# Four plain blocks ahead of the first causal one, and x carried between its two blocks through DRAM

## The chip, the core and the metric

The kernel runs on one core of a Trainium2 chip. The metric is the device time of one execution in microseconds. The program has five engines that run side by side and meet at semaphores: TensorE (PE, with its weight loads listed as PEld), VectorE (DVE), ScalarE (ACT), GpSimd (POOL) and SyncE (SP), which here does nothing but issue DMAs and wait for what they need.

## The reference

The input x has 8 batch elements of 512 rows by 256 columns. Each element passes through two blocks of the same form:

```
x = x + attention_a(layernorm(x))     # 16 heads of 16, all 512 keys, with biases
x = x + tree_ffn(layernorm(x))
x = x + attention_b(layernorm(x))     # 16 heads of 16, rotary, causal, no biases
x = x + tree_ffn(layernorm(x))
```

The tree layer projects to 255 gates, multiplies the branch probabilities of a binary tree of 8 levels into 256 leaf weights, and multiplies those with a matrix of leaf values and an output matrix (folded into one matrix, as are the gates' two, when the kernel opens). Elements do not depend on each other. The first two lines are a *plain* block here, the last two a *causal* block: its scores exist only on and below the diagonal, so it has fewer columns to compute.

## The kernel before, in words

**Phases.** The work is 16 phases, one a block: 8 plain and 8 causal. causal(n) and element(n) (L151 to L160) say what phase n is. With AHEAD = 3 the order is P P P C P C P C P C P C P C C C: phases 0, 1, 2 are the plain blocks of elements 0, 1, 2; phases 3, 5, 7, 9, 11 are causal blocks of elements 0 to 4; phases 4, 6, 8, 10, 12 are plain blocks of elements 3 to 7; phases 13, 14, 15 are the causal blocks of elements 5, 6, 7.

**Slots.** A phase has 64 slots; in each, every engine does its share of one step: PE one block of scores by key (L1104), ACT its exponential (L750, 512 columns or fewer when causal), PE a product with the values (L1128, in fours). Scores for the row maximum (PE L1082, DVE L842 when plain, L838 when causal) run 28 slots ahead (LEAD), so phase n's slots 36 to 63 compute the maxima of phase n + 1, and PE cannot start on them before the stacked queries and keys of n + 1 have landed.

**Work around the slots.** Beside the slots of phase n runs work of other blocks, each step at a due slot of hand-written tables. FINISH (L73) ends block n - 1: its attention output is turned, projected out and added to x (project_out, slots 18 to 23), then layernorm (slots 21 to 28), gates, tree, and the second addition (mix, slots 58 to 63). PREPARE (L85) begins a block m: the layernorm steps (moments, spread, normalize, turn_normed, slots 37 to 55) in phase m - 2, and its heads, splits into three bf16 parts and stacks (slots 1 to 23) in phase m - 1. The split parts are moved into q_stack and k_stack by SP: 12 DMAs for a plain block (L494), 24 for a causal one (L492). SP also sends 4 small rows four times a phase (send_shift, L481, slots 6, 22, 38 and 54). Every engine walks the same tables in program order, so a wait on SP holds all its later DMAs.

**Late blocks.** A causal block of an element needs the output of its plain block, whose mix ends at slot 63 of the phase after it. ready_late(m) (L173) names the blocks for which the input is not there at slot 37 of phase m - 2, or that have no such phase: m = 1, 3 and 15. For them LATE (L108) puts the layernorm steps at slots 0 to 8 of phase m - 1, the heads at slots 9 to 20, and every other step but values 9 slots later (LATE_BY).

**Buffers of x.** x_in takes the input of a plain block for its layernorm, loaded at slot 10 of phase m - 2 (load_x, L455); x_again takes it once more for the addition, loaded at slot 40 of phase m (load_again, L462, for plain blocks), and gets the output bias on POOL (bias_input, L664, plain blocks only). Results are added into x_plain or x_causal by DVE (L900). Between its two blocks an element stays on chip: move (L534) copies x_plain to x_moved, keep (L548) copies x_moved to x_kept, the keep at slot 24 (KEEP_SLOT) and the move at slot 31 (MOVE_SLOT) of phases 4, 6, 8, 10, 12, with two more moves and one more keep after the first two mixes: 7 moves and 6 keeps. A causal block's layernorm reads x_moved (x_plain when late), its addition x_kept. A causal block's result is stored by SP after its mix (L591).

```
FINISH = (
...
    ("mix", 0, (58, 59), 60), ("mix", 1, (61, 62), 63),
PREPARE = (
    ("moments", 0, (), 37 - SLOTS), ("moments", 1, (), 38 - SLOTS), ("spread", 0, (), 39 - SLOTS),
...
LATE = {
    ("moments", 0): ((), 0), ("moments", 1): ((), 1), ("spread", 0): ((), 1), ("normalize", 0): ((), 3),
```

## Time and profile before

| | |
|---|---|
| time, median of 3 runs (lowest, highest) | 1221.77 us (1220.28, 1222.41) |
| time of the profiled execution | 1224.61 us |
| its span, first to last instruction | 1222.9 us |
| mean granted TensorE clock | 0.957 |
| busy share of the span | PE 91%, DVE 76%, ACT 59%, POOL 25% |
| DMA packets' time as a share of 16 engines | q1 22.6% |
| all DMA traffic | 67121 packets, 75.33 MB |
| longest waits in total | POOL L655 for ACT 462.1 us, ACT L750 for PE L1104 420.7 us, DVE L838 for PE L1082 124.4 us |

A window row holds a stretch in us from the span's start, its length, then the busy time of PE, PEld, DVE, ACT and POOL, each with the number of instructions, then the granted TensorE clock (1.00 is full), the share of the DMA engines and GB/s. The windows used are the phases: phase n begins at the start of exponential number 64 n (L750), which cuts the span at 55.0, 132.6, 206.4, 297.6, 363.2, 435.1, 502.2, 574.5, 640.1, 712.0, 777.6, 849.5, 916.1, 987.5, 1055.9, 1137.9 and ends phase 15 at 1190.6 us. A third quarter is the stretch from exponential 32 to 48 of a phase. "SPq" is SP's own queue: the time that it spends on issuing the DMAs.

### The profile page before, as it was taken

The page shows a single profiled execution, that of the slowest core. Times are in us where ns is not written, and L with a number is a line of the kernel's source. Part 1 is how long each engine was busy: PE and PEld are TensorE (multiplying, and loading weights), DVE is VectorE, ACT ScalarE, POOL GpSimd, SP SyncE. Part 2 cuts the span into 40 slices and gives each one's busy share as a digit, 9 for nine tenths or more (in the row PEclk, how much of TensorE's full clock was granted, in tenths as well). Part 3 has the DMA queues.
Part 4 walks back from the last instruction along what each step waited for, and adds up shares of the span by engine and source line. Part 5 has one row for each costly group of instructions (what it writes and reads, how often), then busy time and mean ns, then how long its engine had stood idle before and what let it go on. Part 6 is the DMA issues. An engine that isn't in the chain of part 4 may idle for free.

```text
span 1222.9 us, 18868 instructions
## 1 busy us (share of the span) xinstructions
PE 1112.1 (91%) x6160; PEld 546.0 (45%) x6160; DVE 927.2 (76%) x2599; ACT 720.2 (59%) x1457; POOL 302.7 (25%) x324
## 2 busy tenths in 40 slices
PE   6589999969999998999999998999999998897986
PEld 3133353434544454444544454444544444443544
DVE  3568778657888879797898869797888867774834
ACT  3056765546647775576747774676747665554551
POOL 3011101321315022331315122331315143261210
PEclk9589999989999999999999999999989999987988
DMA  7322220131403240041403241041402212021000
GB/s 207 65 69 70 63 58 21 35 91 48 105 1 101 74 108 16 18 139 35 104 2 95 79 95 28 19 138 35 105 1 75 83 42 81 1 64 41 19 8 28
DMA packets 67121, 75.33 MB, mean 62 GB/s; under 512 B 12464, under 2 KB 52816, under 8 KB 67024
## 3 DMA queue, kind: packets, MB, share of 16 engines
q1 hardware_dynamic: 66960, 74.09, 22.6%
q8 instruction: 50, 0.82, 0.3%
q14 instruction: 47, 0.39, 0.1%
q0 software_dynamic: 64, 0.03, 0.0%
HBM read 12.45 MB, written 4.19 MB: 14 GB/s over the span
## 4 chain that ended last, share of the span: by engine, by line
PE 55%; DVE 25%; ACT 6%; SPq 5%; issue 4%; DMA 4%; POOL 1%; DVEq 0%; ACTq 0%; POOLq 0%
PE ps_work L1212 12%; PE ps_out L1128 11%; PE ps_max L1082 10%; PE ps_key L1104 9%; PE ps_work L1237 9%; DVE neg_max L842 7%; SPq L492 4%; DVE ps_max L838 4%; DVE scratch L996 3%; PE ps_work L1183 3%; ACT probs L750 2%; DMA q_stack<-q_part 2%; DVE scratch L968 2%; DVE scratch L999 2%; DVE moments L938 1%
## 5 line engine op out<-in xcount | busy, mean ns | idle before, releaser
L750 ACT ACTIVATE probs<-ps_key 128x512 f32<-128x512 f32 (+3 forms) x1024 | 514.4, 518 | 424.2 <-PE ps_key L1104 420.7
L1082 PE MATMUL ps_max<-k_stack,q_stack 96*128 96x512 bf16 (+3 forms) x1024 | 360.3, 355 | 58.2 <-DMA q_stack<-q_part 25.2
L842 DVE TENSOR_REDUCE neg_max<-ps_max 128x1 bf16<-128x512 f32 x512 | 337.1, 683 | 90.5 <-PE ps_max L1082 89.2
L1104 PE MATMUL ps_key<-q_stack,k_stack 97*128 97x512 bf16 (+3 forms) x1024 | 353.5, 348 | 18.6 <-ACT probs L750 12.8
L838 DVE CUSTOM_DVE_ANT_0 ps_max<-ps_max,mask_b 128x128 f32<-128x128 f32 (+3 forms) x512 | 247.7, 502 | 126.4 <-PE ps_max L1082 124.4
L1082 PEld LDWEIGHTS ps_max<-k_stack,q_stack 96*128 96x128 bf16 x1024 | 100.0, 98 | 327.0 <-DVE neg_max L842 121.3
L1128 PE MATMUL ps_out<-probs,v_ones 128*32 128x512 f32 (+3 forms) x2048 | 236.5, 535 | 0.6 <-POOL probs L655 0.6
L655 POOL TENSOR_SCALAR_AFFINE_SELECT probs<-probs 128x512 f32<-128x512 f32 x128 | 82.9, 648 | 462.8 <-ACT probs L750 462.1
L1104 PEld LDWEIGHTS ps_key<-q_stack,k_stack 97*128 97x128 bf16 x1024 | 101.3, 99 | 140.9 <-ACT probs L750 84.6
L1183 PE MATMUL ps_work<-ident,scratch 128*128 128x128 f32 x384 | 65.7, 298 | 21.5 <-DMA a_v_bias<-in_a_v_bias 9.2
L677 POOL TENSOR_TENSOR rstd<-variance,minus_half 128x4 f32<-128x4 f32 (+1 forms) x34 | 33.2, 975 | 209.2 <-DVE variance L951 177.2
L1128 PEld LDWEIGHTS ps_out<-probs,v_ones 128*32 128x32 f32 x2048 | 40.7, 109 | 75.2 <-issue 67.3
L1212 PE MATMUL ps_work<-gate_w,turned_block 128*128 128x255 f32 x256 | 72.8, 412 | 1.4 <-ACT turned_block L771 1.4
L838 DVE DVE_READ_ACCUMULATOR2_ANT neg_max<- 128x1 bf16 x512 | 72.9, 142 | 0.0
L1183 PEld LDWEIGHTS ps_work<-ident,scratch 128*128 128x128 f32 x384 | 48.8, 152 | 47.2 <-DVE scratch L968 23.8
L1212 PE MATMUL ps_work<-leaf_w,turned_block 128*128 128x256 f32 x256 | 66.4, 383 | 1.4 <-ACT turned_block L771 1.4
L771 ACT ACTIVATE turned_block<-ps_work 128x512 f32<-128x512 f32 x96 | 57.3, 598 | 12.6 <-PE ps_work L1183 12.6
L697 POOL TENSOR_TENSOR scratch<-scratch,cosine 128x512 f32<-128x512 f32 x32 | 43.5, 1360 | 66.8 <-ACT scratch L786 35.8
L717 POOL TENSOR_TENSOR k_part<-scratch,k_part 128x512 bf16<-128x512 f32 x32 | 40.3, 1271 | 73.8 <-ACT k_part L808 73.8
L1212 PEld LDWEIGHTS ps_work<-gate_w,turned_block 128*128 128x128 f32 x256 | 52.4, 209 | 12.1 <-ACT turned_block L771 2.0
L1212 PEld LDWEIGHTS ps_work<-leaf_w,turned_block 128*128 128x128 f32 x256 | 46.1, 191 | 11.6 <-ACT turned_block L771 1.9
L717 POOL TENSOR_TENSOR q_part<-scratch,q_part 128x512 bf16<-128x512 f32 x32 | 38.0, 1190 | 40.4 <-ACT q_part L808 40.4
(83 smaller groups left out, 1200.7 us busy)
## 6 DMA issues: line engine op xcount, KB each, us to landing
k_stack<-k_part SPq DMA_DIRECT2D x48, 256.0 KB
q_stack<-q_part SPq DMA_DIRECT2D x48, 256.0 KB
k_stack<-k_part SPq DMA_DIRECT2D x96, 128.0 KB
q_stack<-q_part SPq DMA_DIRECT2D x96, 128.0 KB
x_in<-in_x SPq DMA_DIRECT2D x8, 512.0 KB, 4.1
q_stack<-shift_rows SPq DMA_DIRECT2D x256, 1.0 KB, 1.7
x_again<-in_x SPq DMA_DIRECT2D x8, 512.0 KB, 4.0
x_moved<-x_plain SPq DMA_DIRECT2D x7, 512.0 KB, 3.0
```

The costliest lines, as they stand in the source:

```text
L655: pool.affine_select(out=tile, in_=tile, compare_op=ALU.is_ge, fill=0.0, base=0, pattern=[[0, GROUP], [1, P]], channel_multiplier=-1)\
L717: pool.tensor_tensor(parts[which][2][:, i, :], rest_of(which, m)[:, i, :], parts[which][1][:, i, :], ALU.subtract).then_inc(on["low"], 1)
L750: act.activation(probs[step % RING][:, j, q0:T], ps_key[slot % 2][:, 0:T - q0], ACT.Exp, scale=SCALE).then_inc(on["exp_done"], 1)
L771: act.activation(dst[:, :, 2 * P * i:2 * P * i + 2 * P], bank[:, :].rearrange("p (k n) -> p k n", k=KC), ACT.Copy).then_inc(on["turned"], 1)
L838: dve.tensor_tensor_reduce(out=src, in0=src, in1=mask_b[:, T - keys:], scale=-1.0, scalar=-MASKED, op0=ALU.add, op1=ALU.min, accum_out=dst)\
L842: dve.tensor_reduce(out=dst, in_=src, axis=AX_X, op=ALU.max, negate=True)\
L1082: pe.matmul(dst[:, 0:keys], q_stack[n % 2][0:SPLIT_ROWS, h, P * qt:P * qt + P], k_stack[n % 2][0:SPLIT_ROWS, h, 0:keys], start=True, stop= ...
L1104: pe.matmul(ps_key[slot % 2][:, 0:T - q0], k_stack[n % 2][0:STACK_ROWS, h, P * kb:P * kb + P], q_stack[n % 2][0:STACK_ROWS, h, q0:T], star ...
L1128: last = pe.matmul(ps_out[COLS * j:COLS * j + COLS, q0:T], v_flat[n % 2][:, at:at + COLS], probs[step % RING][:, j, q0:T], start=(kb == 0) ...
L1183: last = pe.transpose(by_tile(bank)[:, k, P * t:P * t + P], src[:, 2 * i + t, P * k:P * k + P], ident[:, :])
L1212: last = pe.matmul(by_tile(bank)[:, t, 0:width], turned[:, k, tile], weight[:, k, 0:width], start=(k == 0), stop=(k == KC - 1))
L1237: last = pe.matmul(bank[:, :], weight[:, k, P * i:P * i + P], turned_heads[:, k, :], start=(k == 0), stop=(k == KC - 1))
```

## The change

AHEAD becomes 4, so the order is P P P P C P C P C P C P C C C C: phases 0 to 3 are the plain blocks of elements 0 to 3, phases 4, 6, 8, 10 causal blocks of elements 0 to 3, phases 5, 7, 9, 11 plain blocks of elements 4 to 7, phases 12 to 15 causal blocks of elements 4 to 7. ready_late(m) holds for m = 1 alone. x_moved and x_kept are gone with their copies. After each plain mix SP writes x_plain to the scratch tensor spill in DRAM; a causal block loads its x from there, into x_in at slot 10 of phase m - 2 (behind a wait for every write issued so far) and into x_again at slot 40 of phase m. DVE waits for x_again, in place of x_kept, before it adds a causal block's projection, and for the write before it overwrites x_plain.

```diff
--- before.py
+++ after.py
@@ -62,7 +62,7 @@
 PHASES = 2 * BATCH
-AHEAD = 3
+AHEAD = 4
@@ -113,8 +113,6 @@
 }
 LATE_BY = 9
-KEEP_SLOT, MOVE_SLOT = 24, 31
 PREPARE_FIRST = (
     ("moments", 0), ("spread", 0), ("normalize", 0), ("moments", 1), ("spread", 1), ("normalize", 1),
     ("turn_normed", 0), ("turn_normed", 1), ("heads_k", 0), ("heads_k", 1), ("high_k", 0), ("heads_q", 0),
...
@@ -172,7 +170,7 @@
 def ready_late(m):
-    return m in (1, AHEAD, PHASES - 1)
+    return m == 1
 def prepare_work(m):
@@ -315,8 +313,7 @@
         x_in = sb("x_in", [P, TILES, D])
         x_again = sb("x_again", [P, TILES, D])
         x_plain = sb("x_plain", [P, TILES, D])
-        x_moved = sb("x_moved", [P, TILES, D])
-        x_kept = sb("x_kept", [P, TILES, D])
+        spill = nc.dram_tensor("spill", (BATCH, T, D), F32, kind="Internal").ap()
         x_causal = sb("x_causal", [P, TILES, D])
@@ -353,7 +350,7 @@
         def staged(i, n):
-            room = (x_kept, x_causal)[i // 2][:, 2 * (i % 2):2 * (i % 2) + 2, :].rearrange("p t n -> p (t n)")
+            room = (x_plain, x_causal)[i // 2][:, 2 * (i % 2):2 * (i % 2) + 2, :].rearrange("p t n -> p (t n)")
             return room[:, 0:KC * n].rearrange("p (k n) -> p k n", k=KC)
         normed_block, tanh_gates, leaf_probs = tiles_of(0), tiles_of(0), [tiles_of(1), tiles_of(2)]
@@ -436,13 +433,13 @@
         def stream(m, n):
-            if n >= m:
-                return x_causal if causal(m) else x_plain
-            return x_in if not causal(m) else x_plain if ready_late(m) else x_moved
-        def kept(m):
-            return x_kept if m < PHASES - 2 else x_moved if m < PHASES - 1 else x_plain
+            if n < m:
+                return x_in
+            return x_causal if causal(m) else x_plain
+        def source(m):
+            return spill if causal(m) else x
         @block.sync
         def _(sp):
@@ -457,14 +454,18 @@
                 if count.some("normed"):
                     sp.wait_ge(on["normed"], count.of("normed"))
                     sp.nop(nofuse=True)
-                sp.dma_start(x_in[:, :, :], one(x, element(m))).then_inc(on["x_loaded"], DMA)
+                if causal(m):
+                    sp.wait_ge(on["spilled"], count.of("spilled") * DMA)
+                    sp.nop(nofuse=True)
+                sp.dma_start(x_in[:, :, :], one(source(m), element(m))).then_inc(on["x_loaded"], DMA)
             def load_again(m):
                 if count.some("x_ready"):
                     sp.wait_ge(on["x_ready"], count.of("x_ready"))
                     sp.nop(nofuse=True)
-                sp.dma_start(x_again[:, :, :], one(x, element(m))).then_inc(on["x_again"], DMA)
+                sp.dma_start(x_again[:, :, :], one(source(m), element(m))).then_inc(on["x_again"], DMA)
             def send_shift(n, slot):
                 n, unit, g, _, _ = score_unit(n, slot)
@@ -531,30 +532,6 @@
             def normalize(m, i, n, bank):
                 count.add("normed")
-            def move():
-                sp.wait_ge(on["x_ready"], count.of("x_ready"))
-                sp.nop(nofuse=True)
-                sp.wait_ge(on["normed"], count.of("normed"))
-                sp.nop(nofuse=True)
-                if count.some("kept"):
-                    sp.wait_ge(on["kept"], count.of("kept") * DMA)
-                    sp.nop(nofuse=True)
-                sp.dma_start(x_moved[:, :, :], x_plain[:, :, :]).then_inc(on["moved"], DMA)
-                count.add("moved")
-            def keep():
-                sp.wait_ge(on["x_ready"], count.of("x_ready"))
-                sp.nop(nofuse=True)
-                sp.wait_ge(on["moved"], count.of("moved") * DMA)
-                sp.nop(nofuse=True)
-                sp.dma_start(x_kept[:, :, :], x_moved[:, :, :]).then_inc(on["kept"], DMA)
-                count.add("kept")
             def core(n, slot):
                 for at in lead_slots(n, slot):
                     send_shift(n, at)
@@ -564,25 +541,22 @@
                         count.add("keyed_full", SLOTS)
                     else:
                         load_x(1)
-                if slot == 10 and n + 2 < PHASES and not causal(n + 2):
+                if slot == 10 and n + 2 < PHASES:
                     load_x(n + 2)
-                if slot == 40 and not causal(n):
+                if slot == 40:
                     load_again(n)
-                if 0 < n < PHASES - AHEAD and causal(n - 1):
-                    if slot == KEEP_SLOT:
-                        keep()
-                    if slot == MOVE_SLOT:
-                        move()
             def project_out(m, i, n, bank):
                 count.add("x_ready")
             def mix(m, i, n, bank):
                 count.add("x_ready")
-                if i == 1 and m == 1:
-                    keep()
-                if i == 1 and m < 2:
-                    move()
+                if i == 1 and not causal(m):
+                    sp.wait_ge(on["x_ready"], count.of("x_ready"))
+                    sp.nop(nofuse=True)
+                    sp.dma_start(one(spill, element(m)), x_plain[:, :, :]).then_inc(on["spilled"], DMA)
+                    count.add("spilled")
                 if causal(m) and (i == 1 or alone(n)):
                     sp.wait_ge(on["x_ready"], count.of("x_ready"))
@@ -602,6 +576,8 @@
             sp.sem_inc(on["stored"], DMA)
             count.add("stored")
+            sp.sem_inc(on["spilled"], DMA)
+            count.add("spilled")
             load_x(0)
             for name in FIRST:
                 load_weight(sp, name, first_loaded)
@@ -662,10 +638,12 @@
                 pool.tensor_tensor(two, two, row, ALU.add).then_inc(on["biased"], 1)
             def bias_input(m, i, n, bank):
+                if i == 0:
+                    count.add("x_again")
                 if not causal(m):
                     if i == 0:
-                        pool.wait_ge(on["x_again"], count.next("x_again") * DMA)
+                        pool.wait_ge(on["x_again"], count.of("x_again") * DMA)
                         pool.nop(nofuse=True)
                     add_bias(x_again, i, "a_o_bias")
@@ -901,37 +879,30 @@
                 count.add("x_ready")
             def project_out(m, i, n, bank):
+                if i == 0:
+                    count.add("x_again")
                 if i == 0 and causal(m):
-                    dve.wait_ge(on["kept"], count.of("kept") * DMA)
+                    dve.wait_ge(on["x_again"], count.of("x_again") * DMA)
                     dve.wait_ge(on["stored"], count.next("stored") * DMA)
                 elif not causal(m):
                     dve.wait_ge(on["biased"], count.next("biased"))
-                    if i == 0 and count.some("moved"):
-                        dve.wait_ge(on["moved"], count.of("moved") * DMA)
-                add(m, i, bank, kept(m) if causal(m) else x_again)
-                if i == 1 and causal(m) and n < PHASES - AHEAD:
-                    count.add("kept")
-                    count.add("moved")
+                    if i == 0:
+                        dve.wait_ge(on["spilled"], count.next("spilled") * DMA)
+                add(m, i, bank, x_again)
             def mix(m, i, n, bank):
                 add(m, i, bank, stream(m, n))
-                if i == 1 and m < 2:
-                    count.add("moved")
-                    count.add("kept", m)
             def moments_step(m, i, n, bank):
                 src = stream(m, n)
                 if src is x_in and i == 0:
                     dve.wait_ge(on["x_loaded"], count.next("x_loaded") * DMA)
-                elif src is x_moved and i == 0:
-                    dve.wait_ge(on["moved"], count.of("moved") * DMA)
-                elif n >= m or src is x_plain:
+                elif n >= m:
                     dve.wait_ge(on["x_ready"], count.of("x_ready"))
                 for t in (2 * i, 2 * i + 1):
```

## Rows read from the trace of the kernel before

**Rows 1.** The page, part 1: busy time, share of the span, instructions

```profile
PE 1112.1 (91%) x6160; PEld 546.0 (45%) x6160; DVE 927.2 (76%) x2599; ACT 720.2 (59%) x1457; POOL 302.7 (25%) x324
```

**Rows 2.** Windows, one row a phase or stretch; columns as explained above

```profile
55.00:132.60 77.60, 68.47 (x312) 23.78 (x313) 57.41 (x113) 45.77 (x84) 9.15 (x8) 0.89 0.24 62
132.60:206.40 73.80, 72.21 (x380) 33.16 (x376) 57.38 (x115) 48.52 (x89) 6.92 (x6) 1.00 0.22 51
206.40:297.60 91.20, 77.88 (x396) 35.37 (x392) 63.51 (x172) 51.09 (x96) 20.77 (x17) 0.94 0.18 53
...
297.60:987.50 689.90, 663.70 (x3844) 333.26 (x3840) 575.08 (x1612) 448.93 (x912) 186.72 (x190) 0.99 0.25 66
...
987.50:1055.90 68.40, 61.84 (x384) 32.47 (x376) 50.88 (x180) 39.46 (x92) 28.49 (x30) 0.98 0.18 55
1055.90:1137.90 82.00, 67.89 (x392) 34.74 (x384) 54.46 (x195) 39.97 (x93) 27.19 (x31) 0.85 0.14 39
1137.90:1190.60 52.70, 47.70 (x322) 24.39 (x314) 31.14 (x119) 31.51 (x76) 11.25 (x18) 0.94 0.04 11
```

**Rows 3.** Windows, phases inside the stretch of ten: 3, 5, 11, then 4

```profile
297.60:363.20 65.60, 61.58 (x388) 32.48 (x384) 54.97 (x165) 39.64 (x91) 17.54 (x23) 1.00 0.26 65
435.10:502.20 67.10, 63.08 (x388) 33.14 (x384) 55.22 (x164) 39.69 (x91) 17.52 (x23) 0.97 0.25 56
849.50:916.10 66.60, 63.83 (x388) 33.76 (x384) 55.34 (x165) 39.58 (x92) 17.58 (x23) 0.95 0.24 56
363.20:435.10 71.90, 70.49 (x388) 33.75 (x384) 60.18 (x160) 50.17 (x93) 19.72 (x16) 1.00 0.25 74
```

**Rows 4.** Windows, the third quarters of phases 2, 13 and 14

```profile
254.40:280.90 26.50, 18.38 (x86) 9.03 (x89) 13.24 (x52) 11.45 (x23) 3.60 (x4) 0.81 0.25 73
1023.40:1041.70 18.30, 15.68 (x96) 8.80 (x92) 11.33 (x49) 9.10 (x21) 2.69 (x5) 0.91 0.10 29
1098.30:1123.80 25.50, 17.07 (x88) 9.25 (x91) 11.18 (x49) 9.17 (x23) 4.78 (x6) 0.70 0.22 64
```

**Rows 5.** Chain of waits in order of time: start, us, what, phases 13 and 14

```profile
1023.31 4.45 DMA q_stack<-q_part
...
1103.98 5.73 DMA q_stack<-q_part
```

**Rows 6.** Line L1183, end of phase 1: ns min/median/max

```profile
L1183 PE MATMUL ps_work<-ident,scratch x8: 270/272/273, 190.2 to 194.7; 128*128 128x128 f32 x8
```

**Rows 7.** Tile x_moved, VectorE: the same columns, whole run

```profile
L938 DVE BATCH_NORM_STATS2 moments<-x_moved x24: 383/409/427, 334.2 to 962.2; 128x6 f32<-128x256 f32 x24
...
L968 DVE TENSOR_SCALAR scratch<-x_moved,spread,rstd x24: 394/398/414, 348.6 to 973.4; 128x256 f32<-128x256 f32 x24
```

**Rows 8.** Timeline of SP, phase 13: start, us, line, what, how many

```profile
988.40 0.39 SPq L591 DMA_DIRECT2D out<-x_causal  x1
...
1002.74 10.40 SPq L492 DMA_DIRECT2D k_stack<-k_part  x12
...
1019.85 4.07 SPq L492 DMA_DIRECT2D q_stack<-q_part  x6
```

**Rows 9.** Timeline of SP, phase 3: the last stack of a plain block

```profile
313.27 4.97 SPq L494 DMA_DIRECT2D q_stack<-q_part  x6
```

**Rows 10.** Timeline of SP, phase 4, the load of x for phase 6

```profile
373.97 0.53 SPq L460 DMA_DIRECT2D x_in<-in_x  x1
```

**Rows 11.** DMA view: issues, KB each, median us to landing

```profile
x_in<-in_x SPq DMA_DIRECT2D x8, 512.0 KB, 4.1
...
x_moved<-x_plain SPq DMA_DIRECT2D x7, 512.0 KB, 3.0
out<-x_causal SPq DMA_DIRECT2D x7, 512.0 KB, 2.9
x_kept<-x_moved SPq DMA_DIRECT2D x6, 512.0 KB, 4.8
```

**Rows 12.** Waits of the DMA queue's own engine: total us, times, longest us

```profile
SPq L544 <- DMA x_kept<-x_moved: 24.7, 6, 5.6
```

More of the change, by code:

```diff
@@ L146 @@
     "rotated", "high", "rest", "middle", "low", "values_full", "values_ready", "stacked0", "stacked1",
-    "x_loaded", "x_again", "moved", "kept", "stored",
+    "x_loaded", "x_again", "spilled", "stored",
 )
```

## The prediction

> **What bounds the kernel now.** I read the busy shares first: PE is busy for 1112.1 us, 91% of the span [rows 1], so the question is what it does in the rest. The windows cut by phase answer it [rows 2, 3]. A phase P-then-P (a plain phase whose prepared successor is plain) takes 73.8 us and PE is busy for 72.2 of them; P-then-C takes 71.9 with 70.5 busy; C-then-P 65.6 with 61.6; C-then-C 68.4 with 61.8. The first two are full of PE work. Two phases stand out: phase 2, also P-then-C, takes 91.2 us, and phase 14, C-then-C, 82.0. Phases 3 and 15 are prepared late in exactly those. Their third quarters show the place: 26.5 us at a granted clock of 0.81 and 25.5 us at 0.70, where phase 13 takes 18.3 at 0.91 [rows 4]. The chain of waits says why: at slot 36, where the scores of the next phase begin, PE waits for the last q stack to land, 5.73 us on the chain in phase 14 [rows 5]. Phase 13 has such a wait too, 4.45 us, although it is on time [rows 5]: SP issues 24 stack DMAs and 4 small ones from 1002.74 to 1023.92 with hardly a gap [rows 8]. So the bound is PE in the plain phases, and the chain of the stacks up to slot 36 where a causal block is prepared.
>
> **The change, part by part.** The sum goes phase by phase, in window lengths.
>
> *Order and late steps.* Before: phase 0 (77.6), P-P 73.8, late P-C 91.2, then ten phases in 689.9 us (five C-P, five P-C), C-C 68.4, late C-C 82.0, and phase 15 in 52.7 [rows 2]. They sum to 1135.6. After, with AHEAD = 4: phase 0, two P-P (1, 2), P-C (3), four times C-P and P-C (4 to 11), three C-C (12, 13, 14), phase 15. There are again five P-C but four C-P, so the ten phases become nine: 689.9 less one C-P. Three of the five C-P take 65.6 us, the other two 67.1 and 66.6 at clocks of 0.97 and 0.95 [rows 3]; I take the mean, 66.1, and keep 623.8.
>
> *Work that moves.* The two late blocks' layernorms go to slots 37 to 55 of the phase before, where rows of that kind are without it: P-P phase 1 and C-C phase 13 (380 and 384 matmuls, against 388 in a phase with it) [rows 2, 3]. What a set adds to PE is 8 transposes of 0.272 us [rows 6], 2.2 us; DVE gets 4 statistics of 0.409 and 4 normalizations of 0.398, 3.2 us [rows 7]. In phase 1 PE has 1.6 us to spare, so the set is paid in full; in C-C the last quarter is where it falls, and I charge it there too. The other end is 0 where it fits in gaps, and 5.4 us (2.2 + 3.2) where PE stands for DVE as well. So P-P with a set is 76.0, twice; C-C with a set 68.4 + 2.2 = 70.6, twice (12, 13); phase 14 has no block two ahead and costs 68.4. After: 77.6 + 152.0 + 623.8 + 141.2 + 68.4 + 52.7 = 1115.7. **Saved: 19.9 us.** Put otherwise, the ends of the two late stretches give back 19.3 (91.2 against 71.9) and 13.6 (82.0 against 68.4), 32.9 together. Of that, 9 goes to the less even order (a P-P and a C-C with a set in place of a P-C and a C-P: 146.6 against 138.0) and 4.4 to the sets in phases 1 and 13.
>
> *Copies on chip that go.* 13 DMAs of 512 KB. In P-C phases the keep is issued straight behind the last q stack and the move waits for it: SP stood 24.7 us for this in all [rows 12]. Behind it are the shift rows of slot 38 and the load at slot 40, which no engine missed, so the SP time is worth 0. The keep's bytes may slow the last stack; at most that is the 1.4 us that PE idles in a P-C phase [rows 3], five times, 7 us. I take 0, since nearly all of those 1.4 us are short gaps in other places.
>
> *Writes to DRAM that come.* 8 of 512 KB, issued when the mix is done. The store of a causal block is their like: phase 13's is issued at 988.40, 0.9 us into the phase [rows 8], and such a store lands in 2.9 us [rows 11], so at 3.8 us. SP has no other DMA due before slot 6, and the plain phases get on slot 63 only the wait that causal results have already. x_plain is next overwritten at slot 20. Cost 0.
>
> *Loads that come.* 8 more into x_in, 8 more into x_again, 0.53 us of SP each [rows 10] and 4.1 us to land [rows 11]. The load at slot 10 stands 10.8 us into phase 4 (373.97 against 363.2). Where C-P phases get it, it falls between the k and q stacks of a plain block, which are all issued by 318.24, 20.6 us into phase 3 [rows 9]; scores of the next phase begin some 36 us in, so 15 us cover it. In C-C phases it falls before the k stack, which begins 15.2 us in [rows 8]. The x_again load at slot 40 has 44 slots until the addition. Cost 0; without the cover, 0.5 us in each of phases 11, 12 and 13, so 1.6. The DMA engines carry 11 more transfers of 512 KB, 5.5 MB beside the 75 of before.
>
> *Against the runs.* The profiled execution took 1224.61 us for a span of 1222.9. The sum is a difference within that execution: 1224.6 - 19.9 = 1204.7. The median is 2.8 us below the profiled time, so 1221.8 - 19.9 = 1201.9, said as **1202**.
>
> **The rivals.**
>
> *A: PE has more room than its busy time shows.* Busy PE rows overlap, and the four sets of transposes would vanish between other matmuls: 8.8 us more saved, 1193. Against it: phase 1 sits at 72.2 busy of 73.8; for it: P-C phases carry 388 matmuls in less time than P-P does 380. The Trainium skill, Perfetto Trace Analysis, section Identifying the Most-Contended Engine, holds that matmul busy time does not tell how near TensorE is to its limit and wants the share of weight loads instead. That share is 45% here, so by the rule A would be the forecast; the row by row fit of phase length to busy time speaks against it.
>
> *B: slower, by the spill wait on SP.* load_x(m) of a causal block waits for the newest write in the middle of SP's program, and in phases 11 and 13 the k stack of a causal block is queued behind it. There every us of SP past 15.2 makes the q stack later and is paid at slot 36. The write would have to land later than 14.7 us into the phase (15.2 less 0.5) before this costs anything, against 3.8 by the rows; and to turn the saving of 19.9 round, 10 us later still in both. At 12 us in both, 24 - 19.9 gives 1226. The Trainium skill, DMA: Bandwidth & Descriptors, section on the anatomy of one DMA, warns that a completion can be surprisingly long in coming when the target is HBM. Here stores to DRAM land in 2.9 us where a copy on chip takes 3.0 or 4.8 [rows 11], so this trace does not show it.
>
> *C: the C-C phases are worse when there are three in a row.* Their wait at slot 36 grows, and a third quarter goes the way of phase 14's: 25.5 against 18.3 [rows 4]. One such phase of the three costs 7.2 us (1209), two 14.4 (1216). For it: the stack chain has no slack there, and moments steps come in while DVE catches up. Against: phase 13 finishes a plain block, with POOL's bias additions in front of its products; 13 and 14 will finish causal ones, without.
>
> *D: block 15 is in effect still late.* If its x is not in x_in by slot 37 of phase 13, phase 14 stays near 82.0 and 13.6 us of the saving are gone: 1215.5. The load is issued by slot 10 there and takes 4.1, so little speaks for it.
>
> **How the numbers follow.** The forecast has 0.70, with its own spread of 1196 to 1207 (up to 7 us of gain from the keeps, 3.2 more for one or two of the sets). A has 0.12, C 0.12, D 0.03, B 0.03. The range is 1194.5 to 1210: it takes in the forecast, most of C with one bad phase and the near edge of A, and leaves out B, D and two bad phases. A measurement of this kernel can tell about 0.2%, 2.4 us, from no change. Only B is slower or near even: faster 0.96, same 0.01, slower 0.03.
>
> **What would show it.** Right: phases 2 and 14 near 76 and 68 us with no third quarter above 19; phases 1, 2 at 388 matmuls and 76.0; phases 12 and 13 at 70.6; C-P and P-C as before; SP's waits for the spill near nothing; PE's waits for q_stack short in 12 to 14. Wrong: phases 1 and 2 at 74 (A); the k stack beginning after 16 us in 11 or 13, behind a spill wait (B); a third quarter above 22 us at a clock under 0.85 in 12 to 14 (C); DVE waiting for x_in in phase 13 (D).

## The result, and the profile after

The changed kernel takes **1192.99 us** (median of 4 runs, 1191.32 to 1194.64) against 1221.03 for the kernel before (4 runs): a ratio of 0.9775 with a 95% interval of 0.9751 to 0.9798, so 2.0 to 2.5% faster, about 27.5 us. I had said 1202, saved 19.9. The direction was right; the time lies 1.5 us below my range.

A quarter's clock of 0.91 or the like is a mean: part of the stretch was granted 1.2 GHz and the rest 2.4. Such a part is called a dip below (in before's phase 13 the stretch from 1028.2 to 1031.4 us stands at 0.50 in the windows).

First the windows of the changed kernel, cut by phase as in [rows 2]: phases 1 and 2 (P-P), 3 (P-C), 4 to 11 in one row, 12, 13, 14 (C-C) and 15.

```profile
132.60:208.70 76.10, 74.09 (x388) 34.31 (x384) 61.29 (x128) 49.47 (x91) 9.15 (x8) 0.98 0.24 56
208.70:284.90 76.20, 73.00 (x388) 34.00 (x384) 61.99 (x129) 49.61 (x92) 9.19 (x8) 1.00 0.27 63
284.90:357.80 72.90, 71.48 (x388) 33.77 (x384) 60.07 (x159) 50.10 (x94) 19.18 (x15) 1.00 0.23 66
...
909.20:976.30 67.10, 61.01 (x390) 32.37 (x384) 53.79 (x193) 40.38 (x94) 29.42 (x31) 1.00 0.23 72
976.30:1043.20 66.90, 61.38 (x392) 33.37 (x384) 54.24 (x195) 40.42 (x93) 28.85 (x31) 0.97 0.24 72
1043.20:1108.40 65.20, 59.23 (x384) 31.58 (x376) 50.99 (x182) 39.35 (x91) 27.74 (x30) 1.00 0.22 66
1108.40:1160.90 52.50, 47.44 (x322) 24.15 (x314) 31.25 (x119) 31.53 (x76) 11.33 (x18) 0.93 0.07 21
```

There is no late stretch left: nothing like the 91.2 and 82.0 us of [rows 2]. Phases 4 to 11 run from 357.8 to 909.2, 551.4 us. The P-P phases are where the sum had them (76.0). The C-C phases are not: 67.1, 66.9 and 65.2 against 70.6, 70.6 and 68.4. The phases sum to 1105.5 us where I had 1115.7.

Their third quarters, which answer to [rows 4]:

```profile
945.10:961.70 16.60, 14.13 (x96) 7.91 (x96) 13.07 (x58) 9.10 (x21) 3.73 (x6) 1.00 0.21 70
1011.30:1027.50 16.20, 14.13 (x96) 7.92 (x92) 13.08 (x58) 9.11 (x22) 3.74 (x6) 1.00 0.21 67
1078.20:1094.30 16.10, 14.07 (x96) 7.92 (x92) 11.31 (x49) 9.05 (x21) 2.66 (x5) 1.00 0.20 64
```

All three are at full clock, where before's phase 13 took 18.3 us at 0.91 [rows 4]. The wait at slot 36 is still there (chain of waits in order of time; start, us, what; answers to [rows 5]):

```profile
945.73 3.61 DMA q_stack<-q_part
...
1078.05 3.86 DMA q_stack<-q_part
```

PE's own share of it is short now. Its waits for that stack (total us, times, longest) in the third quarters of before's phase 14 and of the changed kernel's phases 12, 13 and 14:

```profile
PE ps_max L1082 <- DMA q_stack<-q_part: 7.5, 1, 7.5
```

```profile
PE ps_max L1053 <- DMA q_stack<-q_part: 1.4, 1, 1.4
...
PE ps_max L1053 <- DMA q_stack<-q_part: 1.0, 1, 1.0
...
PE ps_max L1053 <- DMA q_stack<-q_part: 0.9, 1, 0.9
```

The new transfers (DMA view; KB each, median us to landing; answers to [rows 11]), and SP in phase 13, the one C-C phase in which a fresh write stands in front of the k stack (timeline; answers to [rows 8]):

```profile
spill<-x_plain SPq DMA_DIRECT2D x8, 512.0 KB, 2.9
x_in<-spill SPq DMA_DIRECT2D x8, 512.0 KB, 7.3
x_again<-spill SPq DMA_DIRECT2D x8, 512.0 KB, 4.0
```

```profile
977.22 0.37 SPq L558 DMA_DIRECT2D spill<-x_plain  x1
983.32 2.40 SPq L482 DMA_DIRECT2D q_stack<-shift_rows  x4
985.87 0.47 SPq L461 DMA_DIRECT2D x_in<-spill  x1
```

The write is issued 0.9 us into the phase, the load 9.6, and the k stack begins at 990.64, 14.3 in. No engine and no queue waits for spill or for x_in from spill anywhere in the lists of waits; the median load from spill into x_in took 7.3 us, not 4.1, and delayed no one.

### The profile page after: what moved, and what is told of

It reads as the page before. It is cut to its first block, busy times and chain, and to the rows that moved or that the text cites. A ratio compares the mean times of both kernels' runs of the same rounds, so it can differ in the third digit from the quotient of the medians.

```text
span 1192.9 us, 18880 instructions
## 1 busy us (share of the span) xinstructions
PE 1100.3 (92%) x6160; PEld 543.7 (46%) x6160; DVE 928.8 (78%) x2599; ACT 720.5 (60%) x1457; POOL 305.3 (26%) x324
## 4 chain that ended last, share of the span: by engine, by line
PE 56%; DVE 26%; issue 5%; ACT 4%; SPq 3%; DMA 2%; POOL 2%; DVEq 0%; POOLq 0%; ACTq 0%
PE ps_work L1183 12%; PE ps_out L1099 12%; PE ps_max L1053 11%; PE ps_key L1075 10%; DVE neg_max L820 8%; PE ps_work L1208 8%; DVE ps_max L816 3%; DVE scratch L967 3%; PE ps_work L1154 3%; DVE scratch L970 2%; SPq L493 2%; ACT probs L728 2%; DVE scratch L939 2%; DMA q_stack<-q_part 2%; DVE scratch L997 2%
## 5 line engine op out<-in xcount | busy, mean ns | idle before, releaser
L1099 PE MATMUL ps_out<-probs,v_ones 128*32 128x512 f32 (+3 forms) x2048 | 234.9, 531 | 0.6 <-POOL probs L631 0.6
L1099 PEld LDWEIGHTS ps_out<-probs,v_ones 128*32 128x32 f32 x2048 | 40.5, 108 | 75.3 <-issue 66.8
L1183 PE MATMUL ps_work<-gate_w,turned_block 128*128 128x255 f32 x256 | 69.0, 395 | 1.4 <-ACT turned_block L749 1.4
L1183 PE MATMUL ps_work<-leaf_w,turned_block 128*128 128x256 f32 x256 | 66.3, 383 | 1.4 <-ACT turned_block L749 1.4
L1183 PEld LDWEIGHTS ps_work<-gate_w,turned_block 128*128 128x128 f32 x256 | 49.5, 198 | 11.0 <-ACT turned_block L749 2.1
L1183 PEld LDWEIGHTS ps_work<-leaf_w,turned_block 128*128 128x128 f32 x256 | 45.9, 190 | 11.5 <-ACT turned_block L749 1.8
```

Source lines behind the costliest of these rows:

```text
L1099: last = pe.matmul(ps_out[COLS * j:COLS * j + COLS, q0:T], v_flat[n % 2][:, at:at + COLS], probs[step % RING][:, j, q0:T], start=(kb == 0) ...
L1183: last = pe.matmul(by_tile(bank)[:, t, 0:width], turned[:, k, tile], weight[:, k, 0:width], start=(k == 0), stop=(k == KC - 1))
```

## Experiments

Ratios are to the kernel before, run on the same chip beside each. The changed kernel was run twice more in this way; its 13 runs have a median of 1193.2 us (1189.7 to 1197.2). In code cuts, `...` stands for lines left out.

**The kernel before, for a second profile.** No edit.

> The kernel before, unchanged, for a second profile. Theory S (the row that priced the causal-to-causal phases was a disturbed one): phase 13's third quarter, 18.3 us at a granted clock of 0.91 in the first profile, comes out nearer 16.6 at 1.00 in another execution, and phase 13 near 66.7 us. Theory R (the wait at slot 36 pulls the clock down every time in the kernel before, and the change ended that): 18.3 at 0.91 again. Time ratio to before 1.00 under both.

Ratio 1.0002 (0.9989 to 1.0015). Windows: phase 13, its second and its third quarter.

```profile
985.80:1052.90 67.10, 61.12 (x384) 32.81 (x376) 51.14 (x180) 39.52 (x92) 28.54 (x30) 0.97 0.19 56
1004.00:1022.10 18.10, 15.60 (x95) 9.85 (x98) 16.40 (x54) 10.26 (x24) 11.62 (x12) 0.91 0.47 141
1022.10:1038.80 16.70, 14.22 (x96) 7.96 (x98) 11.28 (x49) 9.19 (x23) 2.96 (x5) 1.00 0.10 29
```

The third quarter is 16.7 at full clock, as theory S had it, but the dip has only moved a quarter up, where it cost 0.4 us. In the five profiles that I have with the old order, phase 13 has a dip each time (68.4, 67.1, 67.1, 68.7, 68.6 us), so "an accident of one execution" goes too far, and so does theory R: a quarter at 0.91 comes every time, and where it falls decides what it costs: 1.7 us in the third quarter, as in three of the five, and 0.4 in the second, as in two. Without it the phase is 18.2 + 17.7 + 16.7 + 14.1 = 66.7 us, 1.7 below the row I had used.

**Old order, x through DRAM**, twice.

```diff
-AHEAD = 4
+AHEAD = 3
...
-    return m == 1
+    return m in (1, AHEAD, PHASES - 1)
...
-                return x_in
+                return x_plain if causal(m) and ready_late(m) else x_in
...
-                if slot == 10 and n + 2 < PHASES:
+                if slot == 10 and n + 2 < PHASES and not (causal(n + 2) and ready_late(n + 2)):
...
-                elif n >= m:
+                elif n >= m or src is x_plain:
```

> AHEAD back at 3 with phases 3 and 15 late again (their layernorm reads x_plain as before), x still carried through DRAM. It tells the copies' part from the order's. Theory S: the route of x is worth nothing, phases 2 and 14 at 91 and 82 us, the time within 0.3% of before, 1217 to 1225. Theory R (the DRAM route frees SP and the DMA engines and carries the 8 us that I did not forecast): 1210 to 1214, with shorter P-C phases or a shorter phase 13.

> AHEAD = 3 with x through DRAM once more, in more rounds. If the DRAM route is worth about what the first run of it showed: a ratio of 0.9955 to 0.998, phase 12 at 70.9, phase 2 near 89.6 at a clock of 0.96. If only phase 12's wait is real and the rest of the first run was clock: a ratio of 0.998 to 1.0, and phase 2 back at 91 to 92.

First 0.9968 (0.9954 to 0.9983), 3.8 us less than before; then 0.9990 (0.9974 to 1.0006) in 12 runs. The first was outside what I had allowed either theory and would have been told as "the DRAM route is worth 4 us", had it not been repeated. Of its gain some 1.5 us lay in phase 2, at a mean clock of 0.96 (89.7 us); in the second run that phase was back at 91.2 and 0.94. What stays in both profiles is phase 12, 70.8 and 70.9 us against 71.4 and 71.9 in the two profiles of before. The window of the second run's, and before's wait there (waits of VectorE in phase 12; total us, times, longest):

```profile
911.30:982.20 70.90, 69.80 (x388) 33.94 (x384) 59.19 (x160) 50.06 (x93) 19.99 (x16) 1.00 0.22 68
```

```profile
DVE moments L938 <- DMA x_moved<-x_plain: 1.8, 1, 1.8
```

The move stood behind the keep there, and VectorE waited for it. I had read that group of waits for PE and SP and not for DVE.

**Copies left out of the kernel before.** The keeps and moves of phases 4 to 12 are replaced by raising their semaphores.

```diff
-                sp.dma_start(x_moved[:, :, :], x_plain[:, :, :]).then_inc(on["moved"], DMA)
+                if real:
+                    sp.dma_start(x_moved[:, :, :], x_plain[:, :, :]).then_inc(on["moved"], DMA)
+                else:
+                    sp.sem_inc(on["moved"], DMA)
...
-                        keep()
+                        keep(False)
...
-                        move()
+                        move(False)
```

> The kernel before with the five keeps and five moves of phases 4, 6, 8, 10 and 12 left out (their semaphores are raised by SP at once, and the causal blocks read older values of x; the first two moves and the first keep stay). It prices the copies on chip that I costed at 0. If DVE's wait of 1.8 us for x_moved in phase 12 is all: phase 12 at 70.9 in place of 71.9, the other P-C phases at 72.0, 1 us less in all. If the copies carry the 3.9 us by which the kernel with AHEAD = 3 and DRAM beat the kernel before: 3 to 5 us less. If that was chance: 0.

Ratio 1.0005 (0.9989 to 1.0021); phase 12 is 71.0 us, phases 4, 6, 8, 10 are 71.9, 71.9, 72.0 and 71.9. So the copies cost half a us to one in phase 12, which a whole run does not show, and nothing visible in the other P-C phases. The first two moves and the first keep stayed in and are not priced.

**Late steps back, new order.**

```diff
-    return m == 1
+    return m in (1, AHEAD, PHASES - 1)
```

> The changed kernel with blocks 4 and 15 put on the late slots again, order P P P P C ... C C C C and DRAM kept. If the late preparation is what the change removes: phase 3 from 72.9 to 91 us and phase 14 from 65.2 to 79 to 82, less 2.4 and 1.7 for the layernorm sets that leave phases 2 and 13: 28 to 32 us more, 1221 to 1225. If the gain came from elsewhere (the DRAM route, the order itself), under 15 us more.

1227.7 us, ratio 1.0062 (1.0041 to 1.0084): slower than the kernel before, and 34 us above the changed kernel. Windows of phases 3 and 14, then the third quarter of phase 14:

```profile
283.10:374.30 91.20, 78.89 (x396) 35.44 (x392) 63.83 (x172) 51.31 (x96) 20.78 (x17) 0.93 0.18 53
...
1063.90:1145.30 81.40, 67.53 (x392) 34.61 (x384) 54.52 (x195) 40.04 (x93) 27.25 (x31) 0.87 0.17 53
...
1106.50:1131.20 24.70, 17.52 (x88) 9.69 (x90) 11.06 (x47) 9.06 (x22) 4.66 (x6) 0.70 0.28 86
```

Late preparation costs 18.3 us in phase 3 (91.2 against 72.9) and 16.2 in phase 14 (81.4 against 65.2). That is the gain. Everything else in the change, taken without this gain, costs 8 us. The time is 3 us above the range that I expected: the sets that leave phases 2 and 13 gave 2.4 us back in phase 2 (73.8), but phases 12 and 13 took 69.3 and 67.7 us, with dips in their third quarters.

The wait at slot 36 is only half of that cost. By quarters phase 14 takes 19.9, 22.7, 24.7 and 14.1 us where the changed kernel takes 17.3, 17.7, 16.1 and 14.1, and phase 3 takes 22.2, 25.9, 26.4 and 16.7 where that takes 21.0, 18.1, 17.1 and 16.7. The third quarters, with PE's waits of 6.2 and 6.6 us for the last q stack and clocks of 0.70 and 0.77, carry 8.6 of 16.2 and 9.3 of 18.3 us; the rest is in the first two quarters, into which the late block's steps are packed.

**One more plain block ahead.**

```diff
-AHEAD = 4
+AHEAD = 5
```

> AHEAD = 5: one more P-P and C-C phase in place of a P-C and a C-P, nothing late. By the windows of the changed kernel (76.2 + 67.0 against 71.9 + 66.0) 5.3 us more, 1198. If C-C phases were in truth as dear as I priced them (70.6): 9 us more, 1202. If the order costs nothing (busy times of the engines sum to the same): 1193.

1198.4 us, ratio 0.9826 (0.9812 to 0.9841), phases 5.8 us longer in sum than in the first profile of the changed kernel. The order's price is real and close to the 5.3 from the windows: one P-P and one C-C for a P-C and a C-P. It also confirms the smaller C-C rows against my 70.6: its four are 66.6, 66.4, 68.3 (with a dip) and 65.2 us. Four is the least number ahead at which nothing but block 1 is late; five buys nothing.

**The changed kernel again**, in two sets.

> The changed kernel, unchanged, for a second profile on the chip of the runs beside it. Theory S (the clock dips are an accident of each execution, the lengths at full clock are the kernel's own): C-C phases again near 66.9, 66.5 and 65.2 us, 1191 to 1195 in all, dips of 0.5 to 1.7 us in other phases than in the first profile. Rival: the dips (phases 1, 4, 6, 10, 13) fall in the same phases, because something in these phases causes them. The stretch behind the last exponential is 32.0 us at 0.83 or 29.4 at 0.93 (both were seen), which would explain the two groups of times, 1191.4 and 1194.5.

> The changed kernel as it is, the measure for the three kernels beside it on this chip: 1190 to 1195 us. Theory S again: phase 12 67.1 us at full clock, 13 65.8, 14 65.2, and 1.2 to 1.7 more where a clock dip falls into them.

Ratios 0.9785 (0.9754 to 0.9816) and 0.9798 (0.9776 to 0.9821). Phase 12: 68.3 and 67.6 us, phase 13: 65.9 and 66.7, phase 14: 65.1 and 64.9. Phases 12 to 14 together take 199.2, 199.3 and 199.2 us in the three profiles. Phase 14 was at full clock in all three; a dip fell into phase 13, then 12, then 13. Dips in the C-P phases fell on 4, 6 and 10, then on 4, 6 and 8, then on 4 and 8: phase 4 each time, the others not, so neither theory on them is shown.

**Four small DMAs more ahead of the last q stack**, phases 12 to 14.

```diff
+                        if which == "q" and m > 12:
+                            for _ in range(4):
+                                sp.dma_start(filler[count.of("filled")], minus_half[:, :]).then_inc(on["filled"], DMA)
+                                count.add("filled")
                         stack(m, which, 2)
```

> Changed kernel with four more small DMAs issued by SP ahead of the last q stack in phases 12, 13 and 14, some 2.5 us of SP's time each phase. If the wait at slot 36 has no slack left there, as its chain shows (SP issuing without a gap, PE waiting 0.9 to 1.4 us for the last q stack), each us is paid: 7 to 8 us more than the changed kernel, and more where the longer wait costs clock (third quarters at 0.91 as in phase 13 of before's first profile). If there is slack: under 2 us.

1203.5 us against 1192.6 of the changed kernel beside it (ratios 0.9874 and 0.9785). Third quarters of phases 12, 13, 14:

```profile
946.50:964.40 17.90, 14.14 (x96) 7.92 (x93) 13.08 (x58) 9.11 (x22) 3.75 (x6) 1.00 0.23 66
...
1014.00:1034.60 20.60, 17.03 (x96) 9.50 (x92) 13.14 (x58) 9.05 (x21) 3.64 (x6) 0.83 0.20 52
...
1085.30:1104.00 18.70, 15.72 (x96) 8.94 (x92) 11.34 (x49) 9.08 (x22) 2.70 (x5) 0.91 0.20 56
```

They grow by 1.3, 4.4 and 2.6 us. The four DMAs held SP for 1.9 us a phase, not 2.5, and PE's wait for the last q stack grew by 1.3, 1.5 and 1.0 us (2.7, 2.5 and 1.9 in place of 1.4, 1.0 and 0.9). In phase 12, at full clock, that 1.3 is the whole price; in phases 13 and 14, at 0.83 and 0.91, the quarter grew by more than twice what the wait did. So most of a delay at slot 36 is paid at once, and where a lower clock comes with it, the price is more than double. In all the kernel took 10.9 us more, where I had said 7 to 8 and more with the clock.

**The first k stack in two steps.**

```diff
-                        for c in range(2):
+                        for c in halves:
...
-                    if i == 0:
+                    if i == 0 and not causal(m):
                         return
...
-                    stack(m, which, 0)
+                    stack(m, which, 0, (i,) if causal(m) else (0, 1))
```

> Changed kernel, but the first stack DMAs of a causal block go in two steps: the three of half 0 as soon as its high part is made, the three of half 1 a slot later, where SP now waits for both. It tries the step that bounds causal successors, SP's unbroken run of 28 DMAs up to slot 36. If that run sets the end, it begins 1.1 to 1.4 us earlier and PE's wait of 0.9 to 1.4 us for the last q stack goes in phases 12, 13 and 14: third quarters from 16.6, 16.2, 16.1 to 15.2 to 15.6, and fewer clock dips: 2 to 5 us less than the changed kernel. If the parts themselves come late (the q parts of ScalarE and GpSimd), nothing: within 1 us.

Ratio 0.9807 (0.9785 to 0.9828) beside 0.9798: nothing gained. Phases 13 and 14, undisturbed, are as before (65.8 and 65.6 us, third quarters 16.2 and 16.4); phase 12 took 69.8, with two quarters at 0.90 and 0.91, so there were not fewer dips either. SP in phase 12 (timeline), and its wait for the low part of k (total, times, longest), which is 2.4 us in the changed kernel and was 2.4 in before's phase 13:

```profile
921.15 11.82 SPq L493 DMA_DIRECT2D k_stack<-k_part  x12
933.14 4.02 SPq L493 DMA_DIRECT2D q_stack<-q_part  x6
```

```profile
SPq L528 <- POOL k_part L695: 3.7, 1, 3.7
```

The stack begins 13.9 us into the phase in place of 15.3, and the q stack still at 25.8: what SP gains at the start it waits for GpSimd's low part of k. Phases 13 and 14, at full clock, show the same wait of 3.7 us. So my reading of the run of 28 DMAs as SP's own limit was half right: GpSimd's k part stands in the same chain, and shortening one of the two is no use.

**What a layernorm set costs in P-P: transposes, statistics, and their slot.** Three kernels. In the first 6 of 8 transposes are left out for blocks 3 and 4, in the second half of VectorE's part, in the third the statistics come five slots earlier.

```diff
+                        if few and (k, t) != (1, 1):
+                            continue
...
```

```diff
-                for t in (2 * i, 2 * i + 1):
+                for t in (2 * i,) if n < m and m in (3, 4) else (2 * i, 2 * i + 1):
```

```diff
+        if m in (3, 4) and step in ("moments", "spread"):
+            slot -= 5
```

> Changed kernel with 2 of the 8 transposes of the early layernorm left out for blocks 3 and 4 only, so that 2 of 8 are done (phases 1 and 2; part of their heads' input is left out). It prices a set's PE part in a P-P phase. If PE is the bound, as my sum had it: 6 transposes of 0.272 us, 1.6 us a phase, phases 1 and 2 at 74.6 and the whole 3.3 us less than the changed kernel. If VectorE's part is what costs: under 1 us less.

> Changed kernel with half of VectorE's part of the same two sets left out (2 of 4 statistics and 2 of 4 normalizations, 1.6 us a phase; half of the rows keep older values). If VectorE, busy for 17.2 of 19.9 us in those third quarters and ahead of PE there, sets the pace: up to 1.6 us less in each of phases 1 and 2. If PE is the bound: under 0.5 us in each.

> Changed kernel with the statistics (moments, spread) of the next-but-one block five slots earlier (32 to 34 in place of 37 to 39) in phases 1 and 2. Against the P-P phase without a set, the third quarters are 1.2 to 1.4 us longer, with VectorE at 17.2 of 19.9 us and the transposes not yet begun. If it is VectorE's statistics, landing on top of its row maxima, that make P-P phases 2.4 us longer with a set (not the 8 transposes that I charged), third quarters shrink and second ones grow by less: 0.5 to 2 us less than the changed kernel. If it is PE's transposes: no difference.

Ratios 0.9813 (0.9792 to 0.9834), 0.9791 (0.9762 to 0.9820) and 0.9802 (0.9776 to 0.9829), all within reach of the changed kernel's; the windows tell more. Phases 1 and 2, with few transposes, then with few statistics:

```profile
133.20:209.30 76.10, 73.60 (x382) 33.64 (x380) 61.28 (x128) 49.47 (x91) 9.16 (x8) 0.98 0.24 56
209.30:287.10 77.80, 74.22 (x382) 33.53 (x378) 62.00 (x129) 49.70 (x92) 9.15 (x8) 0.98 0.26 62
```

```profile
131.00:206.60 75.60, 72.78 (x388) 34.05 (x384) 60.27 (x124) 49.48 (x91) 9.15 (x8) 1.00 0.25 57
206.60:282.10 75.50, 72.75 (x388) 34.05 (x384) 60.77 (x125) 49.46 (x92) 9.30 (x8) 1.00 0.27 64
```

Both phases without the transposes have a dip. The first can be compared, since phase 1 of the changed kernel had one in the same place (76.1 us at 0.98, the first row of the windows after): it is no shorter. The second phase cannot (last quarter 20.3 us at 0.92, against 18.8 at full clock). Without half of VectorE's part the phases are 0.5 to 0.7 us shorter at full clock, all of it in the last quarter (18.2 against 18.8), where the normalizations are. Twice that is about half of the 2.4 us that a set costs there. Moving the statistics by five slots changed nothing (76.6 and 76.2 us): a miss.

The other half is in the third quarter, and the traces show it, though no run tests it. That quarter takes 18.6 us without a set (before's phase 1) and 19.7 with it (phase 1 of the changed kernel's third profile), with the same 96 matmuls and PE busy for 17.66 and 17.68 us. PE waits there 1.3 us for a row maximum of VectorE, where it was 0.2; with fewer statistics, and with early ones, it is 1.3 still. VectorE is late by one small product of the tree, which takes 1.3 us in place of 0.2 while GpSimd runs its bias addition. GpSimd has two of these additions a plain block; in before's phase 1 one falls beside the tree (so too in phase 2 of the kernel with the late steps back, 73.8 us without a set), in the P-P phases with a set both do. VectorE and GpSimd, before, then the changed kernel's first profile (timelines of phase 1):

```profile
184.41 1.25 DVE L996 SCALAR_TENSOR_TENSOR scratch<-scratch 128x64 f32<-128x64 f32 x1
185.58 0.21 DVE L999 SCALAR_TENSOR_TENSOR scratch<-scratch 128x64 f32<-128x64 f32 x1
...
184.30 1.27 POOL L662 TENSOR_TENSOR x_again<-x_again,a_o_bias 128x512 f32<-128x512 f32 x1 [19.11 <-DMA x_again<-in_x]
```

```profile
184.42 1.05 DVE L967 SCALAR_TENSOR_TENSOR scratch<-scratch 128x64 f32<-128x64 f32 x1
185.39 1.30 DVE L970 SCALAR_TENSOR_TENSOR scratch<-scratch 128x64 f32<-128x64 f32 x1
...
184.12 2.50 POOL L638 TENSOR_TENSOR x_again<-x_again,a_o_bias 128x512 f32<-128x512 f32 x2 [3.63 <-DMA x_again<-in_x]
```

So the set is not priced by PE's transposes, as my sum had it, but by VectorE, on which PE waits: about half its own work in the last quarter, about half, as the traces have it, the second bias addition that now falls beside the tree.

**Twice the DRAM traffic of x.** A second write, and a second load behind each load of a causal block.

```diff
+                if causal(m):
+                    sp.dma_start(x_in2[:, :, :], one(source(m), element(m))).then_inc(on["x_loaded"], DMA)
...
+                if causal(m):
+                    sp.dma_start(x_again2[:, :, :], one(source(m), element(m))).then_inc(on["x_again"], DMA)
...
+                    sp.dma_start(one(second, element(m)), x_plain[:, :, :]).then_inc(on["spilled"], DMA)
```

> Changed kernel with every transfer of x through DRAM done twice: a second write of 512 KB after each plain mix, a second load (into spare buffers) behind each load of a causal block, 24 more transfers and 24 more issues of 0.4 to 0.5 us on SP; all waits are for both. If the cover holds as I wrote (writes in front of slot 6, loads in front of the k stack): 0 to 2 us more than the changed kernel. If the route is near its limit (load at slot 10 ahead of the k stack in phases 11, 12 and 13, DMA engines at 25%): 5 us or more, and the k stack begins later than 15.2 us into those phases.

Ratio 0.9815 (0.978 to 0.985), beside 0.9785, 4 us more by the medians, but the intervals overlap, and the profiled phases sum to 1107.8 us against 1106.5. Two C-P phases at full clock are 66.4 and 66.6 us where they were 65.6; the k stack began 14.3 us into phase 13, as before. Doubling costs at most a few us, so the single route costs about nothing, but 0 is not shown to the us.

## Why the prediction was right and wrong

*What bounds it.* Right in the main. The late stretches were the loss, and all of the gain is their end: 32.9 us in my sum (19.3 and 13.6), 34.5 in the windows of the kernel with the late steps back (18.3 and 16.2), and 34 to 35 in its time. The chain I gave for it, the wait for the last q stack and the clock behind it, is about half of it; the other half is in the two quarters before.

*Order.* The price of a P-P and a C-C for a P-C and a C-P, 9 in my sum, is 5 to 6: the kernel with five ahead showed it.

*P-P with a set.* Size right (76.0; 76.1 and 76.2), reason wrong, so that the size was luck: VectorE's lateness, not the transposes.

*C-C.* This step failed: "C-C with a set 68.4 + 2.2 = 70.6, twice (12, 13); phase 14 ... costs 68.4". It gave 209.6 us; the profile has 199.2, 10.4 less, and that is the whole of the 10.2 by which the sum missed. The rest of the sum was right within 0.5 us a term. The C-C miss comes apart into four pieces, by quarters:
- 1.7 us three times, 5.1: the one row of its kind had a dip to 0.91 in its third quarter, and I charged the dip to all three. I had the clock in the row and used the mean of several rows for C-P, but there was one row for C-C and I did not take the clock out of it. The row was no stray, three of the five profiles of the old order have it so; what failed is that the changed kernel's phases 12 to 14 had one dip among them in each profile, not three.
- 0.9 twice, 1.8: phase 13 of before follows a plain phase, phases 13 and 14 of the changed kernel follow causal ones. A phase's first 8 slots finish the products with the values of the phase before it. In the first quarter (line L1099, by form; count, busy us, mean ns) phase 12 and phase 13 of the changed kernel have

```profile
L1099 PE MATMUL ps_out<-probs,v_ones 128*32 128x512 f32 x24 | 3.2, 605 | 0.0
```

```profile
L1099 PE MATMUL ps_out<-probs,v_ones 128*32 128x512 f32 x8 | 1.1, 605 | 0.0
```

  (the others are narrower), and the quarters are 18.2 and 17.3 us. The same tail, the other way, makes phase 3 72.9 us where P-C after a causal phase is 71.9.
- 1.8 and 1.6, 3.4: a set in C-C costs 0.4 and 0.6 at full clock, not 2.2 (66.7 without and 67.1 with it after a plain phase; 65.2 and 65.8 after a causal one, the latter from the quarters 17.3, 17.7, 16.2 and 14.6 of the kernel with the k stack in two steps). The kernel with the late steps back, which has no set in phase 13, agrees: its last quarter there is 14.1 us. The last quarter without a set (phase 14) and with it (phase 13 of the kernel with the k stack in two steps):

```profile
1094.30:1108.40 14.10, 13.50 (x100) 7.36 (x92) 10.79 (x40) 7.92 (x20) 2.35 (x5) 1.00 0.01 2
```

```profile
1028.30:1042.90 14.60, 14.31 (x108) 8.15 (x102) 12.03 (x44) 8.90 (x22) 2.38 (x5) 1.00 0.00 0
```

  Eight transposes of 0.27 us add 0.8 us to PE's busy time, not 2.2, since in the records most of their time overlaps that of other matmuls. PE's gaps take 0.3 of that, and the quarter grows by 0.5.
- 1.1, and 1.1 back: third quarters 0.5 to 0.6 below 16.7 in 13 and 14, where PE's wait at slot 36 is 1.0 and 0.9 us and not 1.4, against a dip to 0.97 in phase 13.

*Copies and DRAM.* I had 0 for both. Right within what can be measured: the kernel without the copies is at 1.0005, the old order with DRAM at 0.9968 and 0.9990, so that a gain of 2 to 3 us from the route is not ruled out, and the doubled traffic, 4 us more by the medians, is not clear of noise. The exception that the trace of before had shown is DVE's wait of 1.8 us in phase 12, worth half a us to one.

*Against the runs.* The execution profiled before was on the long side: the kernel before had medians of 1218.5 to 1219.9 in the later sets, where the profiled execution took 1224.6. By the second profile of before (phases 1132.3 us) the phases fell by 26.8.

*The rivals.* A has the measured time, 1193, by luck: its sum wants P-P phases at 74, and they were at 76.1 and 76.2. Its premise that transposes vanish among other matmuls did hold, in C-C for about 3.4 us and in the P-P phase that can be compared; there VectorE made up the time. The Trainium skill's rule under it (Perfetto Trace Analysis, Identifying the Most-Contended Engine: matmul busy time does not tell how near TensorE is to its limit) did better than I allowed: 1.6 us of transposes left out of phase 1 shortened it by nothing. B did not occur: no wait for spill, and writes landed in 2.9 us, as stores had, so the warning of DMA: Bandwidth & Descriptors in the Trainium skill about completions to HBM (in its section on DMAs that GpSimd issues; these are SP's) was not borne out here. C's fear was in place as a mechanism, since a delay at slot 36 is paid, and more where the clock falls, but PE's wait did not grow (1.4, 1.0 and 0.9 us against 1.5 in before's phase 13). D did not occur.

## What to carry to other kernels

When a sum is put together from phases of the kernel before, take the clock out of each row first, and look for a second row of the same kind; where there is just one, more profiles of the unchanged kernel would be worth more than more reading of the first (two at least: three of five had the dip in the same quarter). The rows at full clock are then a floor, to which one puts back the dips that come each time. Ask also what stood in front of the phase: work that laps over a border moves the price of its neighbour. Do not add up the busy time of transposes as a price where other matmuls run beside them. And repeat a surprising ratio of 0.3% before explaining it.

## What the runs showed that I had not expected

The stretch behind the last exponential takes 32, 30.4 or 29.4 us with the same work, and differs in the granted clock: the changed kernel's first and second profile, and the kernel with the copies left out.

```profile
1160.90:1192.90 32.00, 20.25 (x84) 14.76 (x84) 12.95 (x52) 5.20 (x9) 1.80 (x3) 0.83 0.10 33
```

```profile
1161.70:1192.10 30.40, 19.04 (x84) 14.04 (x84) 13.08 (x53) 5.26 (x9) 1.84 (x3) 0.89 0.11 35
```

```profile
1190.60:1220.00 29.40, 17.48 (x84) 12.90 (x84) 12.98 (x53) 5.16 (x9) 1.85 (x3) 0.93 0.11 36
```

The old order with DRAM had both ends in its two profiles, 29.4 us at 0.93 and 32.0 at 0.84: one kernel, 2.6 us apart for that alone. The size of a wait does not decide by itself whether the clock falls after it: PE waited 1.5 us at slot 36 in before's phase 13 and the quarter ran at 0.91, and 2.7 us in phase 12 of the kernel with four more DMAs and it ran at 1.00.

And the slow loads into x_in are slow by their place, not by their source. The median from the scratch tensor was 7.3 us where the loads of x took 4.2, but the one load of x issued among stack DMAs (phase 1) took 8.0, and the load from spill in phase 11, ahead of the stacks, 4.0 (DMA view of the changed kernel, windows 147:158 and 846:853):

```profile
x_in<-in_x SPq DMA_DIRECT2D x1, 512.0 KB, 8.0
```

```profile
x_in<-spill SPq DMA_DIRECT2D x1, 512.0 KB, 4.0
```
